# A three-stage transformer block on one core: the slots of the software pipeline rewritten on every engine

## The chip, the core and the metric

The kernel runs on one core of a Trainium2 chip. Five engines work side by side, each through its own list of instructions in order: TensorE (PE, matrix products and transposes), VectorE (DVE), ScalarE (ACT), GpSimd (POOL) and SyncE (SP), which here only issues DMA transfers. They meet at semaphores: an instruction that waits for one holds up everything behind it on its engine. The metric is the device time of one execution in microseconds (us), median of several runs.

## The reference: what is computed

64 batch rows with 64 latents of width 256 each, and a context of 256 tokens. Three residual stages follow one another:

```
x = x + cross_attention(ctx, layernorm(x), mask)   # 16 heads of 16, bucketed relative bias, softmax over 256 keys
x = x + self_attention(layernorm(x))               # 16 heads of 64, norm again, l2-normed q and k, 2 null keys,
                                                   # ALiBi, causal, softmax over 66 keys, output projection
x = x + ffn(layernorm(x))                          # 256 -> 1024 -> 256, relu, 8 LoRA experts, top 2 by a softmax gate
```

Everything is float32 in and out.

## The kernel before

**Units and stages.** The batch is cut into 32 units of 2 batch rows (128 latents, one per partition). Each unit goes through three stages: x (cross attention), a (self attention), f (feed-forward). The kernel is a software pipeline: iteration i works on stage x of unit i, stage a of unit i-1 and stage f of unit i-2, all mixed. `steps` runs iterations 0 to 2 apart, then a hardware loop, then the last three; iterations 32 and 33 only drain a and f. A period is the time from one iteration to the next.

**What sets the order.** Each engine's program walks over `SLOTS`, a row of slot numbers. The table `SLOT` says for each operation (a function such as `x_k` or `a_exp`) in which slots its instances are issued, for each engine apart; inside a slot a fixed order in the code decides. A slot is not a time: it is only a place in one engine's list. What an operation waits for is written in the function with semaphores and is the same for each order.

**Stage x.** `x_k`, `x_v`, `x_q` project context and latents (float32 operands are split in a high and a low float16 part, so a product is three matmuls, lines 450 to 452). Keys and queries go out to HBM and come back stacked (`stack_k_out`, `stack_q_out`, `stack_k_in`, `stack_q_in` on SP, lines 330 to 346), so that one matmul gives the scores of two heads. Then 16 tiles run through a chain: `x_scores` (PE, L524, into one of two banks), `x_bias` (DVE, L1169, bias and running extremum into one of four buffers S), `x_exp` (ACT, L867), `x_turn_probs` (PE, two transposes, L534, into one of two banks), `x_copy_probs` (ACT, L879) and, for each four tiles, `x_pv` (PE, L550). Score t waits for bias t-2; bias t waits for turn t-4; turn t waits for copy t-2. At the end `x_invert` (DVE, L1178) takes the reciprocals of the sums, `x_turn_inv` (L557) and `x_spread_inv` (L567) turn and spread them, `x_copy_weights` (ACT) fetches them, and `x_merge` (DVE, ACT, DVE) scales the outputs. `x_out` (PE) and `x_residual` (DVE, L1199) close the stage, and begin stage a of that unit in the next iteration.

**Stage a.** `a_stats`, `a_rstd`, `a_norm` twice (DVE, POOL, DVE); `a_turn`, `a_k`, `a_q`, `a_v` (PE); `a_copy_raw` (ACT, copy and square); `a_lengths` (DVE, L1229), `a_length` (POOL, L1543 and the power L1545), `a_unit` (DVE, L1235); transposes `a_turn_kq` (L629), `a_spread` (ACT) and `a_place_keys` (DVE); `a_scores` (L644), `a_bias`, `a_softmax_top`, `a_exp`, `a_softmax_end` (L1271 to L1275), `a_turn_probs` (L654), `a_copy_probs`, `a_pv` (L662), `a_copy_pv`, `a_split_pv`, `a_out`, `a_residual`.

**Stage f.** `f_turn`, `f_z`, `f_route` (DVE, a chain of small instructions), `f_turn_z`, then twice `f_first` (PE), `f_relu` (ACT), `f_second` (PE, DVE), `f_split_hid` (ACT, DVE), and last `f_y` (PE, 24 matmuls) and `f_final` (DVE).

**The order of x before.** Score, bias and exp of tile t stand in slot 2t, turn and copy of tile t in slot 2t+7, so on each engine one tile's step alternates with the next one's, and operations of a and f are put between. The end of an iteration on PE is `x_turn_inv`, a turn, `x_spread_inv`, a turn, `f_y`, the last `x_pv`. On POOL `x_split_ctx` (L1510), which prepares the low half of the next unit's context, comes right behind `x_rstd`.

Of the kernel before, what the change touches and what calls it, by code (L numbers as in the profile page):

```python
# [65 lines left out]
SLOTS = range(-14, 2 * (XTILES + TURN_LAG + PV_LAG))  # L66
SLOT = dict(

    pe_x_k=(-14, -14), pe_x_out=(-14,), pe_x_v=(-14, -6), pe_x_turn=(-14,), pe_a_out=(-10,), pe_x_q=(-14,),
    pe_f_turn=(-1,), pe_f_z=(2,), pe_a_turn=(-8, -6), pe_a_k=(-3, -1), pe_a_q=(3, 3), pe_a_v=(3, 6),  # L70
    pe_a_turn_k=(10, 11), pe_a_turn_q=(13, 14), pe_a_scores=(17, 18),
    pe_a_turn_probs=(25, 25, 25, 25), pe_a_pv=(27, 33), pe_f_turn_z=(7,), pe_f_first=(9, 21),
    pe_f_second=(15, 24), pe_f_y=(41,),

    act_x_copy_k=(-14, -14), act_x_copy_turned=(-14,), act_x_spread_q=(-14,), act_x_copy_v=(-3, 6),
    act_f_copy_turned=(-9,), act_a_copy_turned=(-13, -10), act_a_copy_k=(-7, -7), act_a_copy_q=(-1, -1),
    act_a_copy_v=(5, 7), act_a_spread=(12, 12), act_a_exp=(17, 21), act_a_copy_probs=(22, 22, 22, 22),
    act_a_copy_pv=(38, 38), act_f_exp=(-3,), act_f_copy_z=(4,), act_f_relu=(8, 19), act_f_split_hid=(21, 28),
    act_x_split_ctx=(17,),

    dve_x_residual=(-12,), dve_x_split_turned=(-14,), dve_a_residual=(-9,), dve_x_split_k=(-14, -14),
    dve_x_spread_q=(-13,), dve_f_stats=(-7,), dve_a_stats=(-11, -10), dve_f_norm=(-6,), dve_a_norm=(-11, -8),
    dve_f_split_turned=(-3,), dve_a_split_turned=(-8, 0), dve_a_lengths=(2, 4), dve_a_unit=(8, 10),
    dve_a_place_keys=(10, 12), dve_a_bias=(17, 17, 18, 20), dve_a_softmax_top=(17, 21),
    dve_a_softmax_end=(21, 21), dve_a_split_pv=(38, 41), dve_f_logits=(2,), dve_f_route=(3,),
    dve_f_split_z=(6,), dve_f_second=(15, 21), dve_f_split_hid=(27, 36), dve_f_final=(41,), dve_x_stats=(31,),
    dve_x_norm=(33,), dve_x_inv=(33,), pe_x_turn_inv=(34,), act_x_copy_inv=(35,), pe_x_spread_inv=(37,),
    act_x_copy_weights=(38,),

    pool_f_rstd=(6,), pool_a_rstd=(-1, 0), pool_a_length=(22, 29), pool_x_keep=(-5,), pool_a_keep=(16,),  # L90
# [1548 lines left out]
```

How the kernel before makes its waits and increments, by code:

```python
        def lone(eng, name, u, k):  # L165
            value = at(name, u, k)
            if not isinstance(value, int):
                value = eng.to_reg(value)
                eng.wait_ge(sem["consts"], 16)
            return value
# [127 lines left out]
            def load(u):  # L300
                if seen(u - 1):
                    sp.wait_ge(sem["x_normed"], lone(sp, "x_normed", u - 1, 1))
                if seen(u - 1):
                    sp.wait_ge(sem["x_kept"], lone(sp, "x_kept", u - 1, 1))
                sp.dma_start(x_ld[:], io["x"][bass.ts(u, P), :]).then_inc(sem["x_loaded"], 16)
                if seen(u - 1):
                    sp.wait_ge(sem["mask_scaled"], lone(sp, "mask_scaled", u - 1, 1))
                sp.dma_start(mask32[:], io["mask"][bass.ts(u, 1), :].broadcast_to([32, BU * TK // 4])).then_inc(sem["mask_loaded"], 16)
# [1 line left out]
            def load_ctx(u):  # L311
                if seen(u - 1):
                    sp.wait_ge(sem["ctx_split"], lone(sp, "ctx_split", u - 1, 2))
                if seen(u - 1):
                    sp.wait_ge(sem["v_done"], lone(sp, "v_done", u - 1, 2))
                sp.dma_start(ctxT[:].rearrange("p c b k -> p (c b k)"),
                             io["ctxT"][bass.ts(u, P), :]).then_inc(sem["ctx_loaded"], 16)
# [1 line left out]
            def stack_mask(u):  # L319
                sp.wait_ge(sem["mask_scaled"], lone(sp, "mask_scaled", u, 1))
                if seen(u - 1):
                    sp.wait_ge(sem["scores_done"], lone(sp, "scores_done", u - 1, XTILES))
```

## Time and profile before

| | before |
|---|---|
| median of 3 runs | 1959.19 us (1959.10 to 1961.55) |
| the profiled execution, own time | 1956.26 us |
| its span, first to last instruction | 1954.5 us |
| PE busy | 1642.2 us, 84% |
| DVE busy | 1262.2 us, 65% |
| ACT busy | 1123.1 us, 57% |
| POOL busy | 435.2 us, 22% |
| mean granted TensorE clock | 0.923 of 2.4 GHz |

Busy time of an engine counts the whole duration of an instruction; neighbours on an engine overlap by some tens of ns (on PE by more, as matmuls are pipelined), so what an instruction costs its engine is better read from one start to the next. The granted clock of TensorE has two levels, 1.2 and 2.4 GHz; a mean of 0.94 in a window says that a part of it ran at the lower level.

### The profile page before, as it was taken

How to read it: one execution, taken by the hardware profiler on the slowest of the kernel's cores; microseconds unless marked ns; L12 is line 12 of the kernel's file. 1: busy time of each engine (PE TensorE's matmuls, PEld its weight loads, DVE VectorE, ACT ScalarE, POOL GpSimd, SP SyncE). 2: the span in 40 equal slices, each digit the busy share in tenths (PEclk: the TensorE clock that was granted, in tenths of full speed). 3: DMA queues.
4: the chain of work that ended last, by engine and by line, in shares of the span. 5: the costliest groups of instructions: out<-in, count | busy, mean ns of one | idle time of the engine just before them, and what ended most of it. 6: DMA issues, size and time to landing. Idle time of an engine off the chain costs nothing.

```text
span 1954.5 us, 50646 instructions
## 1 busy us (share of the span) xinstructions
PE 1642.2 (84%) x17315; PEld 1173.9 (60%) x17315; DVE 1262.2 (65%) x3347; ACT 1123.1 (57%) x2993; POOL 435.2 (22%) x557
## 2 busy tenths in 40 slices
...
DMA packets 81195, 109.26 MB, mean 56 GB/s; under 512 B 7480, under 2 KB 63364, under 8 KB 81160
## 3 DMA queue, kind: packets, MB, share of 16 engines
...
q14 instruction: 13, 0.11, 0.0%
...
## 4 chain that ended last, share of the span: by engine, by line
PE 40%; DVE 27%; issue 14%; POOL 10%; ACT 4%; DMA 3%; DVEq 1%; SPq 1%; POOLq 1%; ACTq 0%
PE ps_s L567 5%; POOL a_len L1545 5%; PE ps_t L534 4%; PE ps_f L450 3%; PE ps_f L451 3%; PE ps_f L452 3%; PE ps_o L550 3%; DVE aS L1275 2%; DVE a_sum L1271 2%; DVE a_len L1229 2%; PE ps_a L644 2%; PE ps_a L662 2%; DVE S L1169 2%; PE ps_a L629 2%; PE ps_a L654 2%
## 5 line engine op out<-in xcount | busy, mean ns | idle before, releaser
L879 ACT ACTIVATE pT<-ps_t 128x256 f32<-128x256 f32 x512 | 195.5, 382 | 218.5 <-PE ps_t L534 216.1
L867 ACT ACTIVATE S<-S,x_nmx 128x256 f32<-128x256 f32 x512 | 262.0, 513 | 23.5 <-DVE x_nmx L1169 23.1
L1169 DVE CUSTOM_DVE_ANT_0 S<-ps_s,bias 128x256 f32<-128x256 f32 x512 | 209.4, 418 | 97.3 <-PE ps_s L524 79.0
L534 PE MATMUL ps_t<-ident,S 128*128 128x128 f32 x1024 | 215.3, 296 | 55.2 <-ACT pT L879 44.6
L1545 POOL TENSOR_TENSOR a_len<-a_len,half 128x16 f32<-128x16 f32 x64 | 188.6, 2948 | 9.0
L534 PEld LDWEIGHTS ps_t<-ident,S 128*128 128x128 f32 x1024 | 119.2, 151 | 90.4 <-ACT S L867 66.5
L524 PE MATMUL ps_s<-kst,qst 128*128 128x256 f16 x512 | 142.1, 278 | 32.3 <-DVE x_nmx L1169 21.4
L1138 DVE TENSOR_TENSOR aoT<-ps_a,aoT 128x512 f16<-128x512 f32 x64 | 41.3, 686 | 170.9 <-ACT aoT L967 170.9
L1499 POOL TENSOR_SCALAR x_rs<-x_mv 128x1 f32<-128x1 f32 x32 | 7.3, 229 | 619.8 <-DVE x_mv L1119 619.8
L1517 POOL COPY x_res<-x_ld 128x256 f32<-128x256 f32 x32 | 13.2, 411 | 504.0 <-DVE x L1199 504.0
L567 PE MATMUL ps_s<-x_invT,pick 128*128 128x64 f32 x512 | 106.1, 393 | 20.5 <-ACT x_invT L892 20.5
L567 PEld LDWEIGHTS ps_s<-x_invT,pick 128*128 128x128 f32 x512 | 100.1, 300 | 28.8 <-ACT x_invT L892 28.8
L867 ACT ACTIVATION_READ_ACCUMULATOR S<-S,x_nmx 128x1 f32 x512 | 104.4, 204 | 0.0
L450 PE MATMUL ps_f<-zT,f_loraB 128*128 128x128 f16 x512 | 102.6, 220 | 2.1 <-ACT f_h L994 2.1
L451 PE MATMUL ps_f<-zT,f_loraB 128*128 128x128 f16 x512 | 102.5, 219 | 0.0
L452 PE MATMUL ps_f<-zT,f_loraB 128*128 128x128 f16 x512 | 102.4, 219 | 0.0
L1235 DVE TENSOR_TENSOR a_raw<-a_raw,a_len 128x1024 f32<-128x1024 f32 x64 | 78.2, 1223 | 34.2 <-POOL a_len L1545 34.2
L450 PE MATMUL ps_f<-fT,f_wi 128*128 128x128 f16 x512 | 100.3, 221 | 0.0
L451 PE MATMUL ps_f<-fT,f_wi 128*128 128x128 f16 x512 | 99.7, 220 | 0.0
L452 PE MATMUL ps_f<-fT,f_wi 128*128 128x128 f16 x512 | 99.7, 220 | 0.0
L629 PE MATMUL ps_a<-ident,a_raw 128*128 128x128 f32 x512 | 80.9, 281 | 16.9 <-ACT av L946 10.2
L450 PE MATMUL ps_f<-f_wo,hT 128*128 128x256 f16 x256 | 92.5, 361 | 2.2 <-DVE hT L1367 2.2
...
## 6 DMA issues: line engine op xcount, KB each, us to landing
...
```

The lines of the kernel that those rows point to most:

```text
L450: mm(to, left(0), right(0), start=start, stop=False, **flags)
L451: mm(to, left(0), right(1), start=False, stop=False, **flags)
L452: return mm(to, left(1), right(0), start=False, stop=stop, **flags)
L524: mm(ps_s[t % 2][:, 0:TK], qst[:, pair, b, :], kst[:, pair, b, :], start=True, stop=True)\
L534: last = turn(ps_t[t % 2][:, c * P:(c + 1) * P], S[:, t % S_BUFS, c * P:(c + 1) * P], ident[:])
L567: last = mm(ps_s[1][:, n:n + TQ], pick[:, b * KD + g, h2, :], x_invT[:, h2 * TQ:(h2 + 1) * TQ], start=True, stop=True)
L629: last = turn(ps_a[1 - n][:, j * P:(j + 1) * P], a_raw[:, which, 2 * pair:2 * pair + 2, :].rearrange("p h d -> p (h d)"), ident[:])
L867: go(S[:, t % S_BUFS, :], S[:, t % S_BUFS, :], ACT.Exp, bias=x_nmx[:, t:t + 1], scale=-1.0, accum_out=x_sum[:, t:t + 1]).then_inc(sem["exp ...
L879: go(pT[:, t % PT_BUFS].rearrange("p c m -> p (c m)"), ps_t[t % 2][:, 0:2 * P], ACT.Copy)\
L1169: nc.vector.tensor_tensor_reduce(out=S[:, t % S_BUFS, :], in0=ps_s[t % 2][:, 0:TK], in1=bias[:, pair, :], scale=-1.0, scalar=BIG, op0=ALU. ...
L1235: tt(a_raw[:, which], a_raw[:, which], a_len[:, which, :].unsqueeze(2).broadcast_to([P, AH, AD]), ALU.mult)\
L1545: tt(ln, ln, half[:, 0:AH], ALU.pow).then_inc(sem["a_len"], 1)
```

## The change

All of `SLOT` is written anew, and the x tile loop, which was coded as "slot 2t" and "slot 2t+7", gets entries of its own for each of its 16 tiles on each engine (`pe_x_scores`, `act_x_exp`, `dve_x_bias`, `pe_x_turn_probs`, `act_x_copy_probs`, `pe_x_pv`), and so does `x_merge`. Tiles that share a slot are issued in a run. No operation, wait, buffer or transfer is added or removed, and SP's list is the same.

```diff
-SLOTS = range(-14, 2 * (XTILES + TURN_LAG + PV_LAG))
+SLOTS = range(-14, 43)
 SLOT = dict(
-    pe_f_second=(15, 24), pe_f_y=(41,),
+    pe_x_spread_inv=(41,), pe_x_scores=(2, 3, 3, 6, 6, 11, 12, 19, 19, 23, 24, 24, 26, 36, 38, 38),
+    pe_x_turn_probs=(6, 7, 7, 7, 12, 23, 24, 24, 24, 26, 38, 38, 39, 39, 39, 39), pe_x_pv=(23, 26, 41, 41),
...
                     if do_x:
-                        t = s // 2
-                        if s % 2 == 0 and 0 <= t < XTILES:
+                        for t in due("pe_x_scores", s):
                             x_scores(i, t)
-                        if s % 2 == 1 and 0 <= t - TURN_LAG < XTILES:
-                            x_turn_probs(i, t - TURN_LAG)
-                        if s % 2 == 1 and 0 <= t - TURN_LAG - PV_LAG and (t - TURN_LAG - PV_LAG) % QUAD == QUAD - 1:
-                            x_pv(i, (t - TURN_LAG - PV_LAG) // QUAD)
+                        for t in due("pe_x_turn_probs", s):
+                            x_turn_probs(i, t)
+                        for n in due("pe_x_pv", s):
+                            x_pv(i, n)
```

ACT and DVE are edited in the same way. The order of operations on PE in one full iteration is now: x_k0, x_turn, x_k1, x_out, a_out, x_q, a_turn0, x_v0, x_v1, f_turn, a_turn1, a_k0, f_z, a_k1, a_q0, a_q1, f_turn_z, a_v0, score 0, a_v1, scores 1-2, f_first0, scores 3-4, turn 0, a_turn_k0, a_turn_k1, f_second0, turns 1-3, scores 5-6, turn 4, a_turn_q0, a_turn_q1, scores 7-8, a_scores0, score 9, turn 5, x_pv0, a_scores1, scores 10-11, turns 6-8, f_first1, score 12, turn 9, x_pv1, a_turn_probs0, a_turn_probs1, f_second1, a_turn_probs2, score 13, a_turn_probs3, scores 14-15, turns 10-11, a_pv0, a_pv1, f_y, x_turn_inv, turns 12-15, x_spread_inv, x_pv2, x_pv3.

PE in the loop, before: from the last self-attention product (`ps_a<-a_work,av`) to the first row of `f_y` (`ps_f<-f_wo,hT`).

```order
L662 MATMUL ps_a<-a_work,av 64x64 x16
L534 MATMUL ps_t<-ident,S 128x128 x2
L550 MATMUL ps_o<-pT,v 32x128 x8
L557 MATMUL ps_s<-ident,x_inv 128x128
L528 REGISTER_ALU
L534 MATMUL ps_t<-ident,S 128x128 x2
L567 MATMUL ps_s<-x_invT,pick 128x64 x8
L534 MATMUL ps_t<-ident,S 128x128 x2
L450 MATMUL ps_f<-f_wo,hT 128x256
```

PE in the loop, changed: from the last row of `f_y`, which now comes behind both a_pv, to the first row of the next iteration's `x_k`.

```order
L452 MATMUL ps_f<-f_wo,hT 128x256
L557 MATMUL ps_s<-ident,x_inv 128x128
L534 MATMUL ps_t<-ident,S 128x128 x4
L528 REGISTER_ALU
L534 MATMUL ps_t<-ident,S 128x128 x4
L567 MATMUL ps_s<-x_invT,pick 128x64 x8
L550 MATMUL ps_o<-pT,v 32x128 x16
L274 REGISTER_ALU
L274 COMPARE_AND_BRANCH
L450 MATMUL ps_s<-ctxS,wk 128x512
```

`f_y` moved ahead of `x_turn_inv`, and four turns instead of one stand between `x_turn_inv` and `x_spread_inv`.

DVE at the head of the loop body, before: the first rows of an iteration (qT is the low part of the queries, `x_spread_q`).

```order
L1138 TENSOR_TENSOR xnT<-ps_f,xnT 128x256
L1158 SCALAR_TENSOR_TENSOR kT<-ps_s,kT 128x512 x2
L1152 SCALAR_TENSOR_TENSOR qT<-ps_f,qT 64x4x64 x2
L1199 SCALAR_TENSOR_TENSOR x<-ps_o,x_res 128x256
L1117 BN_STATS a_st<-x 128x6
```

DVE at the head of the loop body, changed (the line numbers are smaller by 2).

```order
L1156 SCALAR_TENSOR_TENSOR kT<-ps_s,kT 128x512
L1197 SCALAR_TENSOR_TENSOR x<-ps_o,x_res 128x256
L1115 BN_STATS a_st<-x 128x6
...
L1156 SCALAR_TENSOR_TENSOR kT<-ps_s,kT 128x512
L1136 TENSOR_TENSOR xnT<-ps_f,xnT 128x256
L1121 TENSOR_SCALAR a_x<-x,a_mv,a_rs 128x256
L1288 SCALAR_TENSOR_TENSOR x<-ps_a,a_res 128x256
...
L1136 TENSOR_TENSOR aT<-ps_a,aT 128x256
L1150 SCALAR_TENSOR_TENSOR qT<-ps_f,qT 64x4x64 x2
L1121 TENSOR_SCALAR f_n<-x,f_mv,f_rs 128x256
```

`x_spread_q`, which releases the queries' way through HBM, moved behind both residuals and the first split of stage a.

ACT in the loop, changed: the exps (`S,x_sum<-S,x_nmx`) and copies (`pT<-ps_t`) of tiles 2 to 4 and 0 to 2; before, they alternate one by one.

```order
L993 ACTIVATE f_h<-ps_f 128x512
L862 REGISTER_ALU
L866 ACTIVATE S,x_sum<-S,x_nmx 128x256
L862 REGISTER_ALU
L866 ACTIVATE S,x_sum<-S,x_nmx 128x256
L862 REGISTER_ALU
L866 ACTIVATE S,x_sum<-S,x_nmx 128x256
L877 REGISTER_ALU
L878 ACTIVATE pT<-ps_t 128x256 x3
L1011 ACTIVATE aqT<-ps_a,a_qk 128x512 x2
```

The copies now come in a run behind three exps.

## Rows read from the trace of the kernel before

**Rows 1.** The DVE timeline: start, duration, engine, line, operation; `x_invert` of three units.
```profile
149.39 0.24 DVE L1178 RECIPROCAL x_inv<-x_sum 128x16 f32<-128x16 f32 x1
204.84 0.24 DVE L1178 RECIPROCAL x_inv<-x_sum 128x16 f32<-128x16 f32 x1
1870.59 0.25 DVE L1178 RECIPROCAL x_inv<-x_sum 128x16 f32<-128x16 f32 x1 [1.32 <-ACT S L867]
```

**Rows 2.** Windows: length, PE, PEld, DVE, ACT, POOL busy, PEclk, DMA.
```profile
208.00:1870.00 1662.00, 1464.30 (x15650) 1054.89 (x15651) 1122.22 (x3011) 997.85 (x2691) 384.66 (x489) 0.94 0.18 53
908.00:953.50 45.50, 41.46 (x480) 29.19 (x480) 34.28 (x99) 32.10 (x87) 11.52 (x17) 1.00 0.23 67
953.50:961.00 7.50, 4.70 (x25) 4.27 (x22) 2.68 (x3) 0.55 (x2) 1.82 (x1) 0.58 0.00 0
```

**Rows 3.** The PE timeline at the end of an iteration; in brackets, idle before and releaser.
```profile
955.69 0.47 PE L557 MATMUL ps_s<-ident,x_inv 128*128 128x128 f32 x1 [2.16 <-DVE x_inv L1178]
...
957.23 3.68 PE L567 MATMUL ps_s<-x_invT,pick 128*128 128x64 f32 x16 [0.64 <-ACT x_invT L892]
...
961.13 0.42 PE L450 MATMUL ps_f<-f_wo,hT 128*128 128x256 f16 x1
961.34 0.42 PE L451 MATMUL ps_f<-f_wo,hT 128*128 128x256 f16 x1
```

**Rows 4.** The PE timeline at the same place of the last unit, at full clock.
```profile
1872.53 2.00 PE L567 MATMUL ps_s<-x_invT,pick 128*128 128x64 f32 x16 [0.64 <-ACT x_invT L892]
...
1874.60 0.27 PE L450 MATMUL ps_f<-f_wo,hT 128*128 128x256 f16 x1
1874.70 0.27 PE L451 MATMUL ps_f<-f_wo,hT 128*128 128x256 f16 x1
...
1877.31 0.65 PE L550 MATMUL ps_o<-pT,v 128*32 128x128 f32 x16
```

**Rows 5.** The timeline of all engines around `x_norm` and `x_split_ctx`.
```profile
953.20 2.12 POOL L1510 TENSOR_TENSOR ctxS<-ctxT,ctxS 128x1024 f16<-128x1024 f32 x1
953.27 2.20 DVE L1123 TENSOR_SCALAR x_n<-x_ld,x_mv,x_rs 128x256 f32<-128x256 f32 x1 [1.15 <-POOL x_rs L1501]
...
955.39 0.24 DVE L1178 RECIPROCAL x_inv<-x_sum 128x16 f32<-128x16 f32 x1
```
**Rows 6.** The DVE timeline, first normalisation of stage a.
```profile
913.63 0.42 DVE L1199 SCALAR_TENSOR_TENSOR x<-ps_o,x_res 128x256 f32<-128x256 f32 x1
...
915.94 0.41 DVE L1123 TENSOR_SCALAR a_x<-x,a_mv,a_rs 128x256 f32<-128x256 f32 x1 [1.14 <-POOL a_rs L1501]
```

**Rows 7.** PE's largest wait over the whole run: total us, times, longest.
```profile
PE ps_s L557 <- DVE x_inv L1178: 66.9, 31, 2.3
```

**Rows 8.** The timeline: queries split and first score (unit 2), x_k and split later.
```profile
162.58 0.86 DVE L1152 SCALAR_TENSOR_TENSOR qT<-ps_f,qT 64x256 f16<-64x256 f32 x2
...
172.99 0.27 PE L524 MATMUL ps_s<-kst,qst 128*128 128x256 f16 x1 [0.52 <-DMA qst<-q_hbm]
...
908.25 0.38 PE L450 MATMUL ps_s<-ctxS,wk 128*128 128x512 f16 x1
...
913.17 0.43 DVE L1152 SCALAR_TENSOR_TENSOR qT<-ps_f,qT 64x256 f16<-64x256 f32 x1
```

**Rows 9.** The ACT timeline: exps and copies back to back.
```profile
951.31 0.51 ACT L867 ACTIVATE S<-S,x_nmx 128x256 f32<-128x256 f32 x1
951.80 0.38 ACT L879 ACTIVATE pT<-ps_t 128x256 f32<-128x256 f32 x1
952.06 0.52 ACT L867 ACTIVATE S<-S,x_nmx 128x256 f32<-128x256 f32 x1
```

**Rows 10.** The POOL timeline: the power of `a_length`.
```profile
926.06 2.93 POOL L1545 TENSOR_TENSOR a_len<-a_len,half 128x16 f32<-128x16 f32 x1
```

**Rows 11.** The DVE timeline: the end of the self-attention softmax, one half.
```profile
943.49 0.69 DVE L1271 TENSOR_REDUCE a_sum<-aS 128x8 f32<-128x528 f32 x1
...
944.46 0.71 DVE L1275 TENSOR_TENSOR aS<-aS,a_sum 128x528 f32<-128x528 f32 x1
```

More of the change, by code:

```diff
@@ new lines @@
+    pe_f_turn=(0,), pe_f_z=(1,), pe_f_turn_z=(2,), pe_f_first=(6, 25), pe_f_second=(7, 31), pe_f_y=(39,),
+    act_x_copy_k=(-14, -14), act_x_copy_turned=(-12,), act_x_spread_q=(-4,), act_x_copy_v=(-3, 0),
+    act_x_split_ctx=(14,), act_x_copy_inv=(39,), act_x_copy_weights=(42,),
+    act_x_exp=(1, 1, 3, 3, 3, 11, 12, 12, 12, 19, 22, 24, 27, 27, 27, 28),
+    act_x_copy_probs=(3, 3, 3, 11, 12, 12, 12, 14, 21, 22, 28, 28, 28, 31, 42, 42), act_x_merge=(42,),
+    act_f_copy_turned=(-3,), act_f_exp=(-2,), act_f_copy_z=(1,), act_f_relu=(3, 22), act_f_split_hid=(23, 27),
@@ new lines @@
+    act_a_copy_turned=(-12, -3), act_a_copy_k=(-3, 0), act_a_copy_q=(0, 0), act_a_copy_v=(1, 1),
+    act_a_spread=(6, 8), act_a_exp=(14, 22), act_a_copy_probs=(24, 24, 27, 27), act_a_copy_pv=(28, 28),
+    dve_x_residual=(-11,), dve_x_split_turned=(-9,), dve_x_split_k=(-14, -10), dve_x_spread_q=(-6,),
+    dve_x_stats=(31,), dve_x_norm=(40,), dve_x_inv=(36,),
+    dve_x_bias=(-5, -4, -4, -3, -2, 5, 5, 5, 5, 8, 22, 26, 26, 26, 27, 28), dve_x_merge=(42,),
+    dve_a_residual=(-8,), dve_a_stats=(-11, -8), dve_a_norm=(-9, -6), dve_a_split_turned=(-8, -6),
```

44 lines of the change are left out of this document (18 added, 26 removed).

## The prediction, made before the changed kernel ran

> **What bounds the kernel now.** I read the busy shares first: PE leads, yet it is idle for a sixth of the span. Then the timeline for the period. `x_invert` starts at 204.84 in unit 2 and at 1870.59 in unit 31 [rows 1]: 29 periods of 57.44 us. So 85% of the time is one pattern, and what the change does to one period decides; start and drain are small.
>
> Third, windows. From 208 to 1870 PE is busy 1464.30 of 1662 us at a mean clock of 0.94 [rows 2]: per period 50.6 us busy and 6.8 us idle. The clock is not spread evenly: 1.00 in the 45.5 us from 908, 0.58 in the 7.5 us behind them [rows 2]. A mean of 0.94 with levels of 0.5 and 1 is 12% at 1.2 GHz, 6.9 us a period. Its cost can be read: `x_spread_inv` takes 3.68 us there and 2.00 in the last unit, which ran it at full clock; matmuls of `f_y` come 0.21 us apart against 0.11 [rows 3, 4].
>
> Fourth, the place where it falls: from 953.5 on PE sits idle 2.16 us for `x_inv`, works half a microsecond, sits 0.64 idle, and the spread and most of `f_y` run at half clock [rows 3]. The `x_inv` it waits for is late because `x_norm` stands ahead of it on DVE and lasts 2.20 us, exactly as long as POOL's `x_split_ctx` (953.20 to 955.32) beside it; a normalisation of the same shape takes 0.41 [rows 5, 6]. Over the run this is PE's largest wait, 66.9 us in 31 times [rows 7].
>
> PE's own work per period at full clock: 41.46 us busy in the window of 45.5 [rows 2], and for what lies outside it the last unit shows 1872.53 to 1877.96, 5.4 us [rows 4], plus `x_turn_inv` and a turn, 0.8: 47.7. So 57.4 = 47.7 work + 2.9 lost to the clock + 6.8 idle. The work can't shrink; 9.7 us a period is all an order can win.
>
> **What the change moves, and its cost.** No instruction is added or removed, so every term is a wait. I went through one full iteration, each engine in its new order, each operation at its start-to-start distance from the trace (exp 0.49, copy 0.26 [rows 9]), 0.05 to 0.15 us for each hand-over. Time 0 is PE's start of x_k0.
>
> *Head.* x_k0, x_turn, x_k1 fill PE to 3.0. `x_merge` needs the last x_pv and ends at 2.2, so x_out follows without a wait, where before x_k, x_turn and x_q covered it. x_out and a_out run to 6.2. `x_residual` starts at 3.9; 2.31 us later [rows 6] a_norm0 can start. a_turn0, x_v0, x_v1 bring PE to 9.95. f_turn waits 0.3 (f_norm is behind x_spread_q on DVE), and a_q1 waits 0.3 for a_copy_k1 on ACT, which stands behind f_exp and x_copy_v1. PE reaches a_v0's end at 18.55.
>
> *Queries.* `x_spread_q` now ends at 9.75, 4.4 us later against x_k0 than before (913.60 against 908.25, 5.35 us behind it [rows 8]). In unit 2 the first score waited for the stacked queries and started 9.55 us after that split had ended [rows 8]. Here the keys are back early, so SP issues their loads at once; 9.1 us, queries in at 18.9. Score 0 waits about 0.4; behind it in PE's queue stands a_v1, and for that ACT's copies. By the unit-2 figure the wait is 0.8. A wait of this kind shifts the whole period; I take 0.4.
>
> *Middle.* The powers (2.93 us each on POOL [rows 10]) end at 21.7 and 25.2; a_turn_k0 comes at 23.2 and a_turn_q0 at 26.6, both free of them; a_turn_q0 itself follows a_unit1 (26.45) by 0.1. Turns 2, 3 and 4 wait for a copy each, because the copies stand behind three exps: 0.5 in sum. Scores 7 and 8 wait 0.3 for f_second and two biases on DVE; a_scores0 waits 0.4 for a_spread; turns 6 and 8 wait 0.35 for copies 4 and 6 behind three more exps. a_turn_probs0 waits 0.9: softmax_end (0.69 and 0.71 and the reciprocal, 1.7 together [rows 11]) stands behind softmax_top of the second half. PE starts a_pv0 at 40.2.
>
> *Tail.* a_pv0, a_pv1, f_y run to 45.2 without a wait. Under them ACT does a_copy_pv, exp 15 (done at 44.0), DVE x_inv at 44.05. So x_turn_inv starts the moment f_y is through: the 2.16 us wait is gone. Turns 12 to 15 need copies 10 to 13, and 14 waits 0.35; they cover ACT's fetch of the turned sums except 0.1. Then 2.0 us of spread and two x_pv: 49.9.
>
> The waits named are 0.3 + 0.3 + 0.4 + 0.15 (f_first0) + 0.5 + 0.3 + 0.4 + 0.35 + 0.9 + 0.35 + 0.1 = 4.05. To these come gaps of about 0.2 us which the trace shows ahead of each x_pv, 0.8. Against the figure of 47.7, which counts the pipelined ends of matmuls as busy, some twelve gaps are each 0.13 us shorter: minus 1.6. Idle 3.3, and with the clock at full, which I expect since it stood at 1.00 all through the 45.5 us from 908, whose gaps are like those I find, none above 1 us: 47.7 + 3.3 = 51.0 us a period, 6.4 less.
>
> Bounds: idle can't be below about 0.5 us, since the ping-pong of two banks leaves some (period 48.2); above, the old idle of 6.8 with the clock at full gives 54.5. I take 3.3 as worked out.
>
> Outside the 29 periods: unit 1 and unit 2 (55.5 us from 149.39 to 204.84 [rows 1]) have the same tail and gain 5 each; the drain from x_inv on loses the spread's wait and `f_y` between the turns and the last x_pv, about 2. Unit 0 is led by the constants' loads, nothing. Sum: 29 x 6.44 = 187, + 10 + 2 = 199. The profiled execution took 1956.26, so 1757; its median is 2.9 above: **1760 us**.
>
> **A rule weighed.** x_norm's 2.20 us beside x_split_ctx against 0.41 alone [rows 5, 6] shows that the two engines can shut each other out. The Trainium skill ("GPSIMD Engine Reference", Key points) says why: GpSimd and VectorE share SBUF interfaces, and a VectorE instruction contends in a two-port mode or with two SBUF inputs. By it the changed order has a collision to fear, told as rival 2.
>
> **Rivals.**
> 1. *The clock still falls once a period.* For it: the tail has little but float32 transposes and the spread, and before it falls there in nearly every unit. Against: it fell after 2.2 us of idleness [rows 3], and the 45.5 us ahead, with the same kinds of work and gaps to 1 us, stand at 1.00. Price: 6.9 us at half clock, busy all through, lose 3.4; x 31: 1866 us.
> 2. *x_split_ctx meets x_inv.* POOL's split follows x_rstd and f_keep and starts 1.65 us after x_stats, at 44.5 in my walk; x_inv starts at 44.05. If x_inv comes 0.5 us later and is held as x_norm was, it starts at 46.6, and x_turn_inv at 46.7 in place of 45.2: 1.5 x 31 = 47, 1807 us. For it: only half a microsecond lies between. Against: no row shows a reciprocal held; the one at 955.39 came behind x_norm.
> 3. *The waits mostly vanish*, because a stall at one place uses up the next: idle 1.0, period 48.7, 1693 us. Against: the waits in the middle depend on ACT and DVE, which a stall of PE doesn't advance.
> 4. *Convoys; slower than before.* Scores start 4.4 us later after x_k0, so sixteen tiles have 31 us from score 0 to the next x_k0, where they had 38. PE passes some 14 places at which it needs ACT or DVE through a queue of three exps or a softmax. If each costs 0.5 us more than walked (one exp out of step) the period is 58.3: 1985 us. It decides from 6.4 us on. Against: ACT has 15 us of slack a period.
> 5. *Nothing changes*, since something I don't see holds 57.4: 1959 us.
>
> **How the numbers follow.** Forecast 0.55, rival 1 0.15, rival 2 0.12, rival 3 0.07, rival 4 0.06, rival 5 0.03, rest 0.02 faster in between. The range has to take in rival 2, and rival 1 at its end: 1715 to 1868, which is periods of 49.5 to 54.7. Left out are rivals 3 to 5. A measurement of this kernel tells 0.2% (4 us) from no change; same is half of rival 5 and a little, 0.02; slower 0.06; faster 0.92.
>
> **What would show it.** `x_inv` 51 us apart; windows of 45 us with PEclk 1.00 and no stretch at 0.5; no wait of `x_turn_inv` for `x_inv`; x_norm still about 2 us, but ahead of nobody; a wait of score 0 for `qst<-q_hbm` in nearly all units, 0.4 us; the wait for `aS` about 0.9 us at a_turn_probs0. Wrong would be: a half-clock stretch per unit (rival 1), a RECIPROCAL of 2 us or a late x_inv (rival 2), a wait for `pT` copies of over 3 us per period (rival 4).

## The result and the profile after

| | before | changed |
|---|---|---|
| median, four runs each on one chip | 1960.37 us (1959.10 to 1971.11) | 1706.67 us (1705.38 to 1707.83) |
| ratio | 1 | 0.8695 (0.8664 to 0.8727) |
| span of the profiled execution | 1954.5 us | 1706.1 us |
| its own time | 1956.26 us | 1707.83 us |
| mean granted clock | 0.923 | 0.962 |

Faster by 13%, 53 us beyond the forecast of 1760, and 8 us below the stated range. The direction came as foretold, and so did what becomes of the largest wait and of the clock; the size didn't.

I read the same views as before. First the DVE timeline of the changed kernel (start, duration, engine, line, operation), the reciprocal of units 0, 1, 2 and 31, which answers [rows 1]:

```profile
96.49 0.25 DVE L1176 RECIPROCAL x_inv<-x_sum 128x16 f32<-128x16 f32 x1 [0.26 <-ACT S L866]
...
152.26 0.25 DVE L1176 RECIPROCAL x_inv<-x_sum 128x16 f32<-128x16 f32 x1 [0.66 <-ACT S L866]
...
202.63 0.25 DVE L1176 RECIPROCAL x_inv<-x_sum 128x16 f32<-128x16 f32 x1 [0.28 <-ACT S L866]
...
1619.27 0.25 DVE L1176 RECIPROCAL x_inv<-x_sum 128x16 f32<-128x16 f32 x1 [0.28 <-ACT S L866]
```

(1619.27 - 202.63) / 29 = 48.85 us a period, 8.59 less than before. 29 x 8.59 = 249 us, and the spans differ by 248.4: the whole gain lies in the repeated pattern, and start and drain together give nothing.

Second, the windows (length; busy PE, PEld, DVE, ACT, POOL; granted clock; DMA), against [rows 2]:

```profile
200.00:1620.00 1420.00, 1347.11 (x15752) 998.38 (x15749) 1114.61 (x3022) 1007.46 (x2708) 413.45 (x495) 1.00 0.21 62
...
941.56:990.42 48.86, 46.34 (x545) 34.31 (x542) 38.35 (x104) 34.67 (x93) 14.20 (x17) 1.00 0.22 62
```

PE is busy 95%: 46.35 us a period and 2.5 idle, where it was 50.6 and 6.8. The clock is 1.00 in this stretch; the half-clock stretch of each tail is gone. (The mean of the whole run, 0.962, is lower because of the start and the drain.)

Third, the end of an iteration, where [rows 3] had the 2.16 us wait. PE, and around it DVE and POOL (start, duration, engine; in brackets idle before and releaser):

```profile
984.74 0.25 DVE L1176 RECIPROCAL x_inv<-x_sum 128x16 f32<-128x16 f32 x1 [0.28 <-ACT S L866]
...
985.06 2.13 POOL L1507 TENSOR_TENSOR ctxS<-ctxT,ctxS 128x1024 f16<-128x1024 f32 x1
...
985.46 1.87 DVE L1121 TENSOR_SCALAR x_n<-x_ld,x_mv,x_rs 128x256 f32<-128x256 f32 x1
...
985.92 0.27 PE L557 MATMUL ps_s<-ident,x_inv 128*128 128x128 f32 x1
...
987.06 0.69 PE L534 MATMUL ps_t<-ident,S 128*128 128x128 f32 x4 [0.43 <-ACT pT L878]
...
987.58 1.90 PE L567 MATMUL ps_s<-x_invT,pick 128*128 128x64 f32 x16
...
989.41 1.08 PE L550 MATMUL ps_o<-pT,v 128*32 128x128 f32 x32
...
990.42 0.39 PE L450 MATMUL ps_s<-ctxS,wk 128*128 128x512 f16 x1
```

`x_norm` is still held through the split, 1.87 us, but now it is ahead of nobody: the reciprocal is done before it. `x_turn_inv` starts without a wait, and the spread takes 1.90 us instead of 3.68.

Fourth, PE's waits over the run (total us, times, longest):

```profile
PE ps_t L534 <- ACT pT L878: 53.4, 96, 10.5
PE ps_s L524 <- DVE x_nmx L1167: 20.5, 8, 15.1
PE ps_a L644 <- ACT aqT L1011: 19.3, 32, 1.0
PE ps_f L450 <- DVE xnT L1136: 17.5, 3, 15.3
PE ps_a L629 <- DVE a_raw L1233: 12.9, 32, 2.5
PE ps_f L683 <- DVE f_n L1121: 9.7, 30, 2.8
PE ps_s L524 <- DMA qst<-q_hbm: 9.2, 2, 8.3
```

The wait for `x_inv`, 66.9 us in [rows 7], fell to 3.5 in 2 times. In one period (941.5 to 990.4) I count three waits for copies of turned tiles, 1.2 us together, 0.6 for the spread queries of the self attention (`aqT`), 0.3 for `a_unit` (`a_raw`), 0.2 for `f_n`. The stacked queries (`qst`) cost nothing: the row names two waits in the whole run, both ahead of unit 2.

### The profile page after: what moved, and what is told of

Same layout as the page of the kernel before. It is cut to its first block, busy times and chain, and to the rows that moved or that the text cites. A ratio compares the mean times of both kernels' runs of the same rounds, so it can differ in the third digit from the quotient of the medians.

```text
span 1706.1 us, 50671 instructions
## 1 busy us (share of the span) xinstructions
PE 1517.1 (89%) x17315; PEld 1115.4 (65%) x17315; DVE 1248.0 (73%) x3347; ACT 1128.3 (66%) x2993; POOL 461.1 (27%) x557
## 4 chain that ended last, share of the span: by engine, by line
PE 55%; DVE 14%; issue 10%; POOL 9%; ACT 6%; DMA 3%; SPq 1%; DVEq 0%; POOLq 0%; ACTq 0%
POOL a_len L1542 7%; PE ps_t L534 5%; PE ps_o L550 4%; PE ps_f L450 4%; PE ps_a L662 4%; PE ps_f L452 4%; PE ps_f L451 4%; PE ps_a L450 4%; PE ps_s L567 3%; PE ps_a L452 3%; PE ps_a L451 3%; PE ps_a L644 3%; DVE a_raw L1233 3%; PE ps_a L654 2%; DVE a_len L1227 2%
## 5 line engine op out<-in xcount | busy, mean ns | idle before, releaser
L534 PE MATMUL ps_t<-ident,S 128*128 128x128 f32 x1024 | 182.1, 285 | 57.6 <-ACT pT L878 53.4
L878 ACT ACTIVATE pT<-ps_t 128x256 f32<-128x256 f32 x512 | 176.3, 377 | 68.5 <-PE ps_t L534 64.0
L1542 POOL TENSOR_TENSOR a_len<-a_len,half 128x16 f32<-128x16 f32 x64 | 210.2, 3285 | 9.0
L534 PEld LDWEIGHTS ps_t<-ident,S 128*128 128x128 f32 x1024 | 113.3, 143 | 93.4 <-issue 47.7
L524 PE MATMUL ps_s<-kst,qst 128*128 128x256 f16 x512 | 121.8, 280 | 33.9 <-DVE x_nmx L1167 20.5
L524 PEld LDWEIGHTS ps_s<-kst,qst 128*128 128x128 f16 x512 | 46.0, 98 | 71.0 <-DVE x_nmx L1167 42.4
L932 ACT ACTIVATE a_raw<-ps_a 128x512 f32<-128x512 f32 x128 | 76.2, 595 | 18.2 <-PE ps_a L452 12.2
L945 ACT ACTIVATE av<-ps_a 64x512 f32<-64x512 f32 x128 | 75.9, 593 | 17.8 <-PE ps_a L452 12.2
L913 ACT ACTIVATE aT<-ps_a 128x256 f16<-128x256 f32 x32 | 12.3, 384 | 112.5 <-PE ps_a L588 112.5
L1540 POOL TENSOR_SCALAR a_len<-a_len 128x16 f32<-128x16 f32 x64 | 16.9, 265 | 253.2 <-DVE a_len L1227 253.2
L1227 DVE TENSOR_REDUCE a_len<-a_work 128x16 f32<-128x1024 f32 x64 | 77.8, 1216 | 8.7 <-ACT a_work L936 8.6
```

What stands on the lines that cost most here:

```text
L524: mm(ps_s[t % 2][:, 0:TK], qst[:, pair, b, :], kst[:, pair, b, :], start=True, stop=True)\
L534: last = turn(ps_t[t % 2][:, c * P:(c + 1) * P], S[:, t % S_BUFS, c * P:(c + 1) * P], ident[:])
L878: go(pT[:, t % PT_BUFS].rearrange("p c m -> p (c m)"), ps_t[t % 2][:, 0:2 * P], ACT.Copy)\
L932: go(a_raw[:, which, 8 * n:8 * n + 8, :].rearrange("p h d -> p (h d)"), ps_a[1 - n][:], ACT.Copy, scale=DOWN).then_inc(sem[copied], 1)
L1227: nc.vector.tensor_reduce(a_len[:, which, :], a_sq[:, which], AX, ALU.add)\
L1542: tt(ln, ln, half[:, 0:AH], ALU.pow).then_inc(sem["a_len"], 1)
```

## The experiments

The kernel before ran beside each of them on the same chip, at 1961 to 1966 us; a ratio is against that neighbour, with its 95% interval in brackets. Periods are taken from the reciprocals of units 2 and 31, as above. Where an expectation speaks of theories, it means the forecast's mechanisms and its rivals.

### What one swap is worth, and what the clock is worth

`b_norm_late`: the kernel before, with `x_norm` behind `x_inv` in DVE's list and nothing else.

```diff
-    dve_x_norm=(33,)
+    dve_x_norm=(34,)
```

> The kernel before, with x_norm one slot later on DVE, so that x_inv comes first and x_norm is held by POOL's x_split_ctx behind it. Theory 1: the wait of 2.16 us and the half-clock stretch both go, about 5.3 us a period, 1805 us. Theory 2: only the wait goes, 2.1 x 29 = 61 us, 1900 us, PEclk still 0.94. Rival: something else in the tail is late next (exp 15, the copies), and less than 1.5 us a period is won, 1915 us or more.

1796.17 us, ratio 0.9152 (0.9121 to 0.9182). The period is (1709.71 - 197.36) / 29 = 52.15.

`b_filler`: the kernel before, the late reciprocal left as it is, ten matmuls of no use ahead of `x_turn_inv`.

```diff
+                            pe.wait_ge(sem["biased"], at("biased", i, XTILES))
+                            for _ in range(10):
+                                mm(ps_s[1][:], wk[:, 0, 0, 0:P], a_wk[:, 0, 0, 0:512], start=True, stop=True)
                             x_turn_inv(i)
```

> The kernel before, with ten extra float16 matmuls of 512 columns (2.1 us at full clock, results thrown away) on PE right ahead of x_turn_inv, in the 2.16 us in which PE waits for x_inv. Theory 1 (the idle time itself lets the clock fall, and the fall costs about 3 us a period on top of the wait): the half-clock stretch goes, the period falls from 57.4 to about 54.3, 29 x 3.1 = 90 us less, 1870 us. Theory 2 (the clock falls because the tail is float32 transposes and the spread, filler or not): PEclk stays at 0.94, no change, 1960 us.

1872.03 us, ratio 0.9529 (0.9496 to 0.9562). Windows from 500 to 1500 of `b_filler`, then of `b_norm_late`:

```profile
500.00:1500.00 1000.00, 913.03 (x10143) 643.81 (x10142) 716.88 (x1922) 636.78 (x1715) 247.52 (x310) 1.00 0.19 55
```
```profile
500.00:1500.00 1000.00, 908.87 (x10381) 655.11 (x10378) 747.51 (x1993) 663.97 (x1791) 254.36 (x323) 1.00 0.20 58
```

Both stand at 1.00. The filler leaves `x_inv` as late as before and still saves 89 us: that is the price of the half clock alone, 2.9 us x 31 = 90 in the forecast; the period fell by 3.0, to 54.47. It also shows that the idle time brings the clock down, and not the kind of work in the tail, which is the same here. The swap saves that and the wait too, 165 us. `b_norm_late` splits its period in 0.9089 x 52.15 = 47.4 busy and 4.75 idle. The change as a whole gains 8.59 us a period; one slot number, put into the old order, gains 5.3.

### Is the reciprocal itself held (rival 2)?

`a_norm_early`: the changed kernel with `x_norm` ahead of `x_inv` again. `a_inv_late`: the reciprocal a few slots later, so that it comes close to POOL's split.

```diff
-    dve_x_norm=(40,)        # a_norm_early
+    dve_x_norm=(36,)
-    dve_x_inv=(36,)         # a_inv_late
+    dve_x_inv=(39,)
```

> The changed kernel with x_norm ahead of x_inv on DVE again. Theory A (what counts is whether POOL's split is running when x_norm starts): x_norm waits for x_rstd, starts about 0.3 us before the split and takes 0.4 us, or is held to the split's end. Held: x_inv 2.4 us later, PE waits 1.3 us behind f_y, 1.3 to 2 us a period, 1755 us; not held: 1710 us. The clock stays at 1.00 in both, since f_y stands before the wait.

> The changed kernel with x_inv behind a_split_pv1 on DVE, so that it starts about 0.5 us after POOL's x_split_ctx. My rival 2: the reciprocal (one SBUF input, SBUF output) is held like x_norm to the split's end, lasts about 1.8 us, PE waits 1.2 us behind f_y and the time rises by 1.3 x 29 = 38 us to 1745. Against: only some forms of instruction are held; the reciprocal takes 0.25 us and the time stays within 0.3% of 1707.

1708.52 us (0.8693, 0.8667 to 0.8718) and 1702.84 us (0.8664, 0.8637 to 0.8690); both periods 48.84 to 48.85, as the changed kernel's. The timeline of `a_norm_early`, DVE and POOL:

```profile
939.51 0.46 DVE L1121 TENSOR_SCALAR x_n<-x_ld,x_mv,x_rs 128x256 f32<-128x256 f32 x1 [0.32 <-POOL x_rs L1498]
...
939.78 2.17 POOL L1507 TENSOR_TENSOR ctxS<-ctxT,ctxS 128x1024 f16<-128x1024 f32 x1
...
939.89 0.24 DVE L1176 RECIPROCAL x_inv<-x_sum 128x16 f32<-128x16 f32 x1
```

Here `x_norm` began 0.27 us before the split and took 0.46 us; the reciprocal ran inside the split in its usual 0.24. In all 32 units of this run the reciprocal took 0.24 to 0.25, so a reciprocal of this size is not held, and rival 2 had no ground. In `a_inv_late` the reciprocal started 0.08 us ahead of the split, so that run says only that the time doesn't hang on its place.

`a_norm_early` says one thing more. With `x_norm` put back in front of `x_inv` the changed kernel loses nothing: there POOL's split comes late enough for `x_norm` to begin ahead of it, and `f_y` covers the rest. So the swap's 5.3 us is its price in the old order, not a share of the new one, and the parts can't be added up.

### The head of the iteration

`b_head`: the kernel before with the changed head (`x_out`, `a_out` early, `x_q`, `x_v` and `x_spread_q` late). `b_head_tail`: that and the tail (`x_norm` behind `x_inv`, `f_y` ahead of `x_turn_inv`). `b_head_tail_q`: that with `a_q` and `a_v0` ahead of the first score.

```diff
-    pe_x_k=(-14, -14), pe_x_out=(-14,), pe_x_v=(-14, -6), pe_a_out=(-10,), pe_x_q=(-14,)
+    pe_x_k=(-14, -8), pe_x_out=(-6,), pe_x_v=(-1, -1), pe_a_out=(-4,), pe_x_q=(-3,)     # b_head
...
-    pe_f_y=(41,), dve_f_split_hid=(27, 36), dve_x_norm=(33,)
+    pe_f_y=(34,), dve_f_split_hid=(27, 31), dve_x_norm=(34,)                            # and b_head_tail
...
-    pe_a_q=(3, 3), pe_a_v=(3, 6), pe_f_turn_z=(7,)
+    pe_a_q=(0, 0), pe_a_v=(0, 1), pe_f_turn_z=(1,)                                      # and b_head_tail_q
```

> The kernel before with the head of the iteration (all slots below 0: projections, residuals, normalisations, splits of the three stages) in the changed kernel's order on PE, ACT, DVE and POOL, while the tile loop, the middle and the tail stay. Theory: the waits of PE for the split of aT (1.0 us) and for f_n (0.4) go, minus 1.2 us a period, 1925 us; the clock still falls in the tail. Rival: the first score now waits for the queries (split 4 us later against x_k0), and nothing is won, 1960 us or more.

> Head as in the run above, and the tail changed too: x_inv ahead of x_norm and f_y ahead of x_turn_inv, f_split_hid ahead of x_inv; tile loop and middle stay. Theory 1: head 35 us and tail 165 us add up, 1760 us, PEclk near 1.00; what is left to 1707 us is the middle with its bursts. Rival: the head's part or the tail's is not additive and the time stays above 1800 us.

> Head and tail changed as in the run that gave 1916 us, and on PE a_q0, a_q1 and a_v0 put ahead of the first score, as the changed kernel has it, f_turn_z and a_v1 right behind. Theory: the loss there is the first score's wait of 2.9 us for the stacked queries; with 4 us of other products ahead of it the wait goes, 3 us a period, 1916 - 90 = 1826 us or less, down to 1770 if the head's other gains show. Rival: the tile loop, which can't be shortened, then starts 4 us later and the end moves with it, 1900 us or more.

2016.79 us (1.0281, 1.0247 to 1.0315), 1915.87 us (0.9762, 0.9731 to 0.9794) and 1945.83 us (0.9897, 0.9864 to 0.9929): three misses. PE's waits in `b_head`, then in `b_head_tail_q`:

```profile
PE ps_s L524 <- issue: 88.1, 28, 4.8
```
```profile
PE ps_a L629 <- DVE akT L1244: 82.3, 32, 3.7
PE ps_s L524 <- DVE x_nmx L1169: 61.6, 69, 5.7
```

The new head makes the queries late, and in the old order the first score comes at once behind them: it waits 3 us a unit ("issue" is the row's name for it; the keys and queries are what it needs). With more work ahead of that score that wait goes, but waits for `akT` (2.6 us a unit) and for biases (1.9, where the kernel before has 0.7) come in its place, and the time is 30 us longer still. Of the orders tried, the new head pays only together with the new loop; which trait of the loop makes it pay, these runs don't separate.

`a_old_head`, the converse: the changed kernel with the head of before.

```diff
-    pe_x_k=(-14, -8), pe_x_out=(-6,), pe_x_v=(-1, -1), pe_x_turn=(-12,), pe_x_q=(-3,)
-    pe_a_out=(-4,), pe_a_turn=(-2, 0), pe_a_k=(0, 1)
+    pe_x_k=(-14, -14), pe_x_out=(-14,), pe_x_v=(-14, -6), pe_x_turn=(-14,), pe_x_q=(-14,)
+    pe_a_out=(-10,), pe_a_turn=(-8, -6), pe_a_k=(-3, -1)
...
```

> The changed kernel with the head of the iteration (everything ahead of f_z and a_q0) in the order of the kernel before on all engines. Theory: the old head has waits for the split of aT (1.0 us) and for f_n (0.4) that the new one hasn't; plus 1.3 us a period, 1745 us. Rival: what the new head wins elsewhere it loses here, since the old one brings the queries 4 us sooner, and the time stays at 1707.

1801.03 us, ratio 0.9173 (0.9140 to 0.9207), period 52.03. Its window from 500 to 1500, and its waits:

```profile
500.00:1500.00 1000.00, 894.92 (x10424) 661.89 (x10423) 743.61 (x2003) 665.62 (x1794) 272.91 (x325) 1.00 0.20 58
```
```profile
PE ps_a L450 <- DVE anT L1136: 36.6, 31, 1.2
PE ps_a L588 <- DVE aT L1136: 31.7, 32, 2.2
...
PE ps_f L697 <- DVE zr L1354: 20.0, 31, 3.9
```

46.56 busy, 5.47 idle. These waits are 1.2 + 1.0 + 0.5; with 0.2 more for `f_n` than in the changed kernel they make 2.9 of the 3.2 us a period that the new head takes away. And the time equals that of `b_norm_late`, which has neither the new loop nor the new tail: 5 us apart, with intervals that overlap. I had expected 1745.

### The loop, the tail, and the queries' way

`a_loop_only`: `a_old_head` with `x_norm` ahead of `x_inv` and `f_y` late, so that of the change mainly the new tile loop and middle are left. `a_fy_late`: the changed kernel with `f_y` last on PE, behind the spread and the last `x_pv`. `b_both`: the kernel before with `x_norm` late and `f_y` early.

```diff
-    dve_x_norm=(40,), pe_f_y=(39,)                              # a_loop_only, on a_old_head
+    dve_x_norm=(36,), pe_f_y=(42,)
-    pe_f_y=(39,)                                                # a_fy_late, on the changed
+    pe_f_y=(42,)
-    dve_x_norm=(33,), pe_f_y=(41,), dve_f_split_hid=(27, 36)    # b_both, on before
+    dve_x_norm=(34,), pe_f_y=(34,), dve_f_split_hid=(27, 31)
```

> The changed kernel with head and tail as near to the kernel before as they go: old head, x_norm ahead of x_inv, f_y last on PE. What stays of the change is the tile loop in bursts and the middle. Theory: loop and middle win nothing by themselves (the kernel before with x_inv first ran 1796 us and the changed kernel with the old head 1801), so the time comes out near the old one: 94 us for the head and 107 for f_y on top of 1707, 1905 us, and up to 1960 if the wait for x_inv grows by x_norm and the clock falls in each unit. Rival: the bursts carry a share of their own, and the time stays under 1870 us.

> The changed kernel with f_y as PE's last operation of an iteration, behind x_spread_inv and x_pv. Theory 1: PE waits about 1.4 us for x_inv and 0.4 more for copies, too little for the clock to fall, so plus 1.8 us a period, 1760 us at PEclk 1.00. Theory 2: a wait of 1.4 us with the thin work behind it is enough for the clock, a half-clock stretch comes back and 3 us more are lost, 1845 us. Rival: the waits hide the ACT work behind them, 1715 us.

> The kernel before with the tail alone changed: x_inv ahead of x_norm (which alone gave 1796 us), and f_y ahead of x_turn_inv with f_split_hid ahead of x_inv. Theory: f_y covers what ACT needs for the copies ahead of the spread less than one thinks, since the waits of 0.64 for the turned sums and 0.47 ahead of the last x_pv stay or go: minus 0.6 us a period, 1778 us. Rival: f_y is early but its place is empty later (x_k waits for the weights), no gain or a loss, 1796 us or more.

| | us | ratio (interval) | period | clock, 500 to 1500 |
|---|---|---|---|---|
| `a_loop_only` | 1993.08 | 1.0159 (1.0128 to 1.0189) | 58.26 | 0.94 |
| `a_fy_late` | 1813.99 | 0.9239 (0.9204 to 0.9274) | 52.47 | 0.97 |
| `b_both` | 1885.12 | 0.9588 (0.9559 to 0.9617) | 55.14 | 0.98 |

PE's waits of each, in this order:

```profile
PE ps_s L557 <- DVE x_inv L1176: 70.2, 32, 5.0
```
```profile
PE ps_s L557 <- DVE x_inv L1176: 54.3, 32, 2.1
...
PE ps_o L450 <- DVE oT L1136: 11.5, 30, 3.0
```
```profile
PE ps_f L501 <- DVE f_out L1374: 42.9, 29, 1.6
```

The new loop with the old head and a late `f_y` wins nothing: it is 31 us slower than before, 1.6%, by an interval that doesn't reach 1. The 31 us are not the loop's price, though. In this run `f_y` comes last of all, where the kernel before has an `x_pv` behind it, and the next `x_turn` then waits for `f_final`, 17.8 us over the run. `a_fy_late` has no x_norm in front of `x_inv` and still waits 1.7 us: nothing but `f_y` covers the exps 14 and 15 and the reciprocal. The clock of 0.97 means 6% at half, 3.1 us a period, of which 1.6 is lost. It doesn't fall every time: of 29 windows of one period each, 16 stand at 1.00 and 13 at 0.90 or 0.93, where in the kernel before, with its 2.2 us wait, all 29 are below 1.00. 1.7 + 1.6 + 0.4 for `oT` is 3.7, and the period grew by 3.6. In `b_both`, 89 us slower than `b_norm_late`, `f_y` early leaves `f_final` at its old place, and the old head's `x_turn` needs the bank that `f_final` reads: 1.5 us a unit. To that come 0.5 for the copy ahead of the last `x_pv`, and the clock, whose 0.98 means 2.2 us at half, 1.1 lost: 3.1 in sum, for a period that is 3.0 longer. The early `f_y` is worth 107 us in the changed kernel, and costs 89 in the old one.

`a_keys_late`: the changed kernel with the second half of the keys split later, so that queries and keys go out together again.

```diff
-    dve_x_split_k=(-14, -10)
+    dve_x_split_k=(-14, -7)
```

> The changed kernel with the second split of the keys (x_split_k1 on DVE) moved behind the split of aT, so that the keys' way out to HBM starts 3 us later and runs beside the queries' way. Theory: the prediction's wait of the first score for the queries (0.4 us) didn't come because the two transfers no longer run together (landing of q_hbm 1.8 us against 2.9 before). Then q_hbm lands in 2.9 us again, the loads behind it start 2 us later, the first score waits about 1.6 us, and the time rises by 45 us to 1752. Rival: there is slack of 2 us or more ahead of the first score, 1707 us.

1730.85 us, ratio 0.8815 (0.8780 to 0.8849), period 49.64. DMA issues (KB each, median us from issue to landing), changed and `a_keys_late`:

```profile
q_hbm<-qT SPq DMA_DIRECT2D x64, 128.0 KB, 1.8
```
```profile
q_hbm<-qT SPq DMA_DIRECT2D x64, 128.0 KB, 2.9
```

PE's waits of `a_keys_late`:

```profile
PE ps_f L683 <- DVE f_n L1121: 27.8, 32, 2.8
...
PE ps_s L524 <- issue: 10.7, 20, 1.2
```

The landing went back to the 2.9 us it had before, and the wait of score 0 came back (10.7 / 32 = 0.3 us a unit). `f_n` is later on DVE, 0.6 us a unit more than in the changed kernel, and the wait for `a_raw` is 0.3 less; with 0.1 of small ones that is 0.7 of the 0.8 us of the period. I had expected 1752.

But the landing is not what made the queries late. The SP timeline, changed (x_k0 at 941.56) and `a_keys_late` (x_k0 at 954.43):

```profile
947.39 0.39 SPq L338 DMA_DIRECT2D k_hbm<-kT  x1
950.03 1.44 SPq L346 DMA_DIRECT2D q_hbm<-qT  x2
...
952.98 1.24 SPq L330 DMA_DIRECT2D qst<-q_hbm  x2
```
```profile
963.82 0.39 SPq L338 DMA_DIRECT2D k_hbm<-kT  x1
964.38 1.41 SPq L346 DMA_DIRECT2D q_hbm<-qT  x2
...
968.07 1.24 SPq L330 DMA_DIRECT2D qst<-q_hbm  x2
```

and SP's wait in `a_keys_late`, 0.7 us in 1 time in the changed kernel:

```profile
SPq L354 <- DMA k_hbm<-kT: 28.5, 31, 1.3
```

SP takes its list in order. The queries' stores stand behind the keys' store and begin 9.95 us after x_k0 instead of 8.47; their loads stand behind the keys' loads, which wait 0.9 us for the keys to land. So the loads of the queries start 13.6 us after x_k0 instead of 11.4, and for the queries' own landing SP hardly waits (0.7 us in the whole run). What spares the changed kernel the wait is that the keys are out of the queries' way on SP; that the stores also land 1.1 us sooner is measured, but no run shows that it counts.

### What holds the last 2.5 us

`a_alternate`: exps and copies of tiles 2 to 8 one by one on ACT. `a_alt_inv`: that and `x_inv` late. `c_turns`: that alternation and the runs of turns on PE broken. `c_turns_inv`: that and `x_inv` late.

```diff
-    act_x_exp=(1, 1, 3, 3, 3, 11, 12, 12, 12, 19, ...), act_x_copy_probs=(3, 3, 3, 11, 12, 12, 12, 14, ...)
+    act_x_exp=(1, 1, 3, 4, 5, 10, 11, 12, 13, 19, ...), act_x_copy_probs=(3, 4, 5, 10, 11, 12, 13, 14, ...)  # a_alternate
-    pe_x_turn_probs=(6, 7, 7, 7, 12, 23, 24, 24, 24, 26, 38, 38, 39, 39, 39, 39), pe_f_y=(39,), pe_x_turn_inv=(39,)
+    pe_x_turn_probs=(6, 6, 7, 7, 12, 23, 24, 24, 26, 26, 38, 38, 39, 39, 40, 40), pe_f_y=(40,), pe_x_turn_inv=(40,)  # and c_turns
...
```

> The changed kernel with ACT's exps and copies of tiles 2 to 8 one by one in turn (exp 2, copy 0, exp 3, copy 1, exp 4, copy 2; exp 5, copy 3, exp 6, copy 4 and so on) in place of three exps and then three copies. My walk of the prediction: PE's turns wait 0.35 to 0.4 us at two places because copies stand behind three exps, so the runs cost 0.7 us a period and 1707 - 20 = 1687 us comes out. Rival: ACT then stands and waits for the turns itself, the exps behind get late, and a_scores0, which waits for a_spread, with them: 1707 us or more.

> The changed kernel with each run of three or four turns on PE broken so that no turn waits for the copy of a turn right ahead of it: turn 1 ahead of a_turn_k0, turn 8 behind f_first1, turns 12 and 13 ahead of f_y, and on ACT copies 10 and 11 ahead of a_copy_pv, exps and copies 2 to 8 in turn. Theory: three waits of 0.39, 0.35 and 0.42 us a period, which the profile shows and my walk had, are real losses: 1.16 x 29 = 34 us, 1670 us. Rival: each is made up at the next wait (a_unit, a_spread, softmax), the period stays at 48.85 and the time at 1703.

> As the run above, and x_inv behind a_split_pv1 on DVE. Theory: the move of x_inv doesn't touch the period (48.85 in the earlier run with it) but shortens the end by 4 us, so 1666 us. Rival: with turns 12 and 13 gone from behind f_y, PE waits for x_inv and the time is 20 us longer than the run above.

> The changed kernel with both small moves that gave 1703 us each: ACT's exps and copies of tiles 2 to 8 in turn, x_inv behind a_split_pv1. Theory: neither touches the period (48.85), both act on start and end alone; at best 1699 us, 0.4% under the changed kernel. Rival: they act on the same end and 1703 us stays.

1702.74 us (0.8671, 0.8645 to 0.8696), 1713.70 us (0.8730, 0.8705 to 0.8755), 1715.51 us (0.8736, 0.8713 to 0.8759), 1704.88 us (0.8677, 0.8653 to 0.8700). None is told apart from the changed kernel by these intervals, and the alternation that I had hoped 20 us from leaves the period at 48.84. But `c_turns` is slower than `a_alternate`, on which it builds: the two intervals don't meet, and its period is 49.24. In `c_turns` the waits for copies fell from 53 to 28.5 us over the run, but those for `a_unit` rose from 12.9 to 25.8, and for the softmax (17.6) and `a_work` (9.7) new ones came: the idle time moved from place to place and grew. The chain of waits of the changed kernel names a candidate, the power:

```profile
POOL a_len L1542 7%; PE ps_t L534 5%; PE ps_o L550 4%; PE ps_f L450 4%; PE ps_a L662 4%; PE ps_f L452 4%; PE ps_f L451 4%; PE ps_a L450 4%; PE ps_s L567 3%; PE ps_a L452 3%; PE ps_a L451 3%; PE ps_a L644 3%; DVE a_raw L1233 3%; PE ps_a L654 2%; DVE a_len L1227 2%
```

`a_nopow` leaves the power out, with a multiplication in its place, so that queries and keys are scaled wrongly and only the time counts, and `c_turns_nopow` does so in `c_turns`.

```diff
-tt(ln, ln, half[:, 0:AH], ALU.pow).then_inc(sem["a_len"], 1)
+tt(ln, ln, half[:, 0:AH], ALU.mult).then_inc(sem["a_len"], 1)
```

> The changed kernel with POOL's two powers of a_length (2.93 and 3.65 us) replaced by multiplications, so q and k of the self attention are scaled wrongly; all else is computed as before. Theory (the period is held by a chain through the second power: a_unit1, a_turn_kq, a_spread, a_scores, softmax): the wait for a_raw (0.34 us) goes and the queries' units come 3 us sooner, 0.3 to 0.8 us a period, 1690 us. Rival: the chain isn't the bound, the later waits stay as they are, 1705 us.

> The kernel with the runs of turns broken up (1714 us), and the powers replaced by multiplications as in the run above. Theory: the breaking up won nothing because the chain through the second power, which starts with its stretched 3.65 us, took each gain back (the wait for a_raw rose from 0.34 to 0.78). Without the powers the turns' gain of 1.1 us shows: 15 us or more under a_nopow, 1675 us. Rival: the new waits (softmax 0.57, a_work 0.32) come from the exps' and copies' new order on ACT, and the time stays above a_nopow.

1688.65 us (0.8602, 0.8576 to 0.8629) and 1686.52 us (0.8588, 0.8561 to 0.8615). The powers are worth 18 us in the changed kernel, and 27 in `c_turns`. The periods say where: 48.85 falls to 48.31, and 49.24 to 48.62, which is 0.54 and 0.62. So the powers take only 0.1 of the 0.4 us a period that the broken turns lose, and without them these are still 0.3 behind; that the medians come out 2 us apart the other way, where I had expected 15, is won ahead of unit 2 (its reciprocal at 197.19 against 202.55). PE's waits of `c_turns_nopow`:

```profile
PE ps_t L534 <- ACT pT L878: 28.9, 35, 10.6
PE ps_s L524 <- DVE x_nmx L1167: 20.4, 8, 17.6
PE ps_a L644 <- ACT aqT L1011: 19.3, 32, 1.0
PE ps_a L654 <- DVE aS L1273: 17.4, 31, 0.6
PE ps_f L450 <- DVE xnT L1136: 16.9, 3, 14.7
PE ps_a L654 <- ACT a_work L958: 9.7, 30, 0.3
```

The waits for the softmax and `a_work` stay, so they come with the new order of turns, exps and copies and not from the powers. What gives them, and so what holds the 2.3 us of idle time that a period has even without the powers (66.2 us in the 1400 from 200 of `a_nopow`, period 48.31), stays open.

## Why the prediction was wrong

**The mechanism, right.** The 2.16 us wait and the half clock were one thing, caused by `x_norm` in front of `x_inv`; the forecast put 5.1 us of the period on it (2.16 + 2.9), and `b_norm_late` measured 5.3. The clock stays at 1.00 from 200 to 1620 us (rival 1 wrong), the reciprocal is not held (rival 2 wrong), no convoy came (rival 4 wrong in this kernel; `b_head_tail_q` shows that waits for DVE of that kind were a real danger for part of the change). What the forecast had to size beside this was the rest: 3.3 us a period from the new order of head, loop and tail, which it put at 1.3.

**The step that failed: the list of waits.** The forecast said "The waits named are [...] = 4.05. To these come gaps of about 0.2 us which the trace shows ahead of each x_pv, 0.8", less 1.6 of shorter tails, on 47.7 of work. Work less tails, 46.1, was nearly right: 46.35 was measured. The waits were put at 4.85 and the idle time is 2.5, and three of them make up 2.1 of that 2.35:
- `a_turn_probs0` 0.9: none. PE came there at 977.62, 0.6 us later than walked, having waited in the middle, and the softmax had ended at 977.57. A wait is used up by those ahead of it, which was rival 3's reason; its 1693 us was nearer than my 1760.
- The gaps ahead of `x_pv`, 0.8: a gap that I had read off the weight loads. PE itself shows none there: in the rows above `x_pv` starts at 989.41, ahead of the modelled end of the spread (987.58 + 1.90), without a bracket.
- Score 0 for the queries, 0.4: none. I had taken 9.1 us for the trip, from the one unit in which the trace before shows that wait [rows 8], where queries and keys go out together. Here the split ends at 951.05, the loads of the queries are issued by 954.22 and land in 4.7: at most 7.9 us, since the keys no longer hold SP (`a_keys_late`).

The walk itself ended at 49.9; the sum that gave the forecast is 51.0. Its check points, in us from x_k0, against the trace:

| | walk | trace | difference |
|---|---|---|---|
| `x_spread_q` ends | 9.75 | 9.49 | -0.26 |
| `a_v0` through, score 0 can start | 18.55 (+0.4 wait) | 18.0 | -0.55, no wait |
| `a_turn_probs0` | 35.5 (+0.9 wait) | 36.06 | +0.56, no wait |
| `a_pv0` | 40.2 | 39.67 | -0.53 |
| next x_k0 | 49.9 | 48.86 | -1.0 |

It was 2% long over a whole iteration. Of the 2.15 us by which the forecast's period is too long, about 1.0 is the walk's own, its waits at score 0 and at `a_turn_probs0` above all, and 1.1 was laid on top of it: the 0.8 ahead of the `x_pv`, which the walk had not produced, and 0.3 by which the busy figure less tails plus the waits doesn't agree with the walk. 2.15 x 29 = 62 us.

**Start and drain.** The forecast gave them 12 us. Unit 2 gained 5.1 as foretold (202.63 - 152.26 = 50.37 against 55.45), but unit 1 gained 1.9 instead of 5, and unit 0's reciprocal comes at 96.49 instead of 91.76, with single waits of 15 us for a bias and 10 for a copy ahead of it, where the kernel before has 1.2 and 5.4 at most; that the runs of tiles have nothing beside them there is my reading, and no run tests it. The drain is 2.9 us longer, at a mean clock of 0.80 instead of 0.90. So the 12 us came out as -0.7: 13 us lost there and 62 won in the periods give the 49 us between 1757 and the 1707.8 of the profiled execution. The two errors pull against each other; with start and drain as foretold the miss would have been larger.

**The range.** Its low end, 1715, meant a period of 49.5. I had derived 48.2 as the least possible and then cut rival 3 away. The bound from the rows would have held the time.

**What the forecast didn't see.** It priced each wait as if the parts of the change stood by themselves. By the runs they don't. Put into the old order, the head costs 55 us, the early `f_y` costs 89 on top of the swap, and loop and middle with the old head and a late `f_y` come out at +31; all together give -254. The swap is the only part tried that pays by itself, and in the finished order it is worth nothing (`a_norm_early`).
